# A state-space scan with routed experts on one Trainium2 core: the fifth expert tile one unit later, and x·D by a matmul with a diagonal matrix

## The reference

```python
xn = layernorm(x)
# state-space part, for each batch
x_dbl = xn @ x_proj_w.T                        # 128 + 16 + 16 columns: delta_un, B, C
delta = softplus(delta_un @ dt_proj_w.T + b)   # (512 tokens, 512 channels)
state = exp(delta * A) * state + delta * B * xn    # scan over tokens, 16 states a channel
y     = sum over the 16 states of state * C
s     = y + xn * D_param                       # D_param: one number for each channel
# experts: the 2 of 8 with the largest gate logits, for each token
g     = silu(mean of relu(xn @ expert_w[e] + expert_b[e]) over the two chosen e)
out   = x + s * g
```

## Time and profile before

| | |
|---|---|
| median of 3 runs | 2082.71 us (2080.89 to 2089.23) |
| the profiled execution | 2084.19 us, of which 2082.5 us are the span from first to last instruction |
| mean granted TensorE clock | 0.943 of full |
| busy share of the span | PE 87%, DVE 90%, ACT 73%, POOL 90% |
| batches 1 to 14 | first scan of batch 1 at 190.3 us, of batch 15 at 1946.9 us: 125.5 us each |

### The profile page before, as it was taken

How to read it: one execution, slowest core, us unless ns; L and a number is a source line. 1 busy time by engine, 2 the same in 40 slices (tenths; PEclk the granted TensorE clock), 3 DMA queues, 4 the chain that set the end, 5 groups by cost and what they waited for, 6 DMA issues and landing times.

```text
span 2082.5 us, 30329 instructions
## 1 busy us (share of the span) xinstructions
PE 1812.1 (87%) x8688; PEld 1189.3 (57%) x8688; DVE 1867.7 (90%) x2596; ACT 1517.1 (73%) x3010; POOL 1866.3 (90%) x1004
## 2 busy tenths in 40 slices
PE   4698998989889798998989989798997989889895
PEld 2465655656556465655656556465655656556563
DVE  4777999898999989999898999989989898999997
ACT  4656768687686867768687696867878677686664
POOL 2958999999899999998999999999998999999996
PEclk8798998999999999998999999999999999999997
DMA  8669899898898979889898997979989898998995
GB/s 312 237 200 367 284 312 356 268 383 260 326 331 275 376 243 384 280 298 351 268 377 261 335 342 257 373 246 384 300 283 362 253 364 277 315 347 272 396 308 143
DMA packets 279350, 640.76 MB, mean 308 GB/s; under 512 B 22272, under 2 KB 22784, under 8 KB 268944
## 3 DMA queue, kind: packets, MB, share of 16 engines
q1 hardware_dynamic: 185776, 446.36, 60.9%
q10 hardware_dynamic: 68832, 125.34, 16.2%
q0 software_dynamic: 24576, 67.13, 11.3%
HBM read 516.58 MB, written 122.16 MB: 307 GB/s over the span
## 4 chain that ended last, share of the span: by engine, by line
PE 34%; ACT 18%; DVE 13%; DMA 13%; issue 13%; POOL 6%; SPq 2%; ACTq 1%; DVEq 0%; POOLq 0%
PE z_ps L1214 17%; DMA xn<-in_x 8%; ACT scan_ps L764 5%; DVE scan_ps L1061 5%; PE y_ps L1230 4%; PE proj_ps L1164 4%; POOL dbx L537 3%; DMA bc_rows<-bc_row 3%; DVE p_sb L1071 3%; DVE h_sb L1061 3%; PE y_ps L1247 2%; PE xt_ps L1199 2%; PE proj_ps L1156 1%; ACT xn L623 1%; ACT tok L635 1%
## 5 line engine op out<-in xcount | busy, mean ns | idle before, releaser
L537 POOL TENSOR_TENSOR dbx<-b_sb,u_sb 128x1024 f32<-128x1024 f32 x512 | 1241.9, 2554 | 73.7 <-DVE u_sb L973 37.8
L1214 PE MATMUL z_ps<-w_sb,xsT 128*128 128x512 f32 x1920 | 913.8, 621 | 47.8 <-ACT r_sb L785 25.0
L1061 DVE TENSOR_TENSOR_SCAN scan_ps<-scan_ps,dbx 128x512 f32<-128x512 f32 x704 | 852.9, 1219 | 90.9 <-ACT scan_ps L764 84.8
L764 ACT ACTIVATE scan_ps<-delta,a_sb 128x512 f32<-128x512 f32 x1024 | 699.0, 687 | 213.0 <-DVE p_sb L1071 196.2
L1214 PEld LDWEIGHTS z_ps<-w_sb,xsT 128*128 128x128 f32 x1920 | 363.8, 200 | 432.4 <-issue 423.0
L1230 PE MATMUL y_ps<-ident,p_sb 128*128 128x128 f32 x2816 | 418.3, 283 | 118.6 <-DVE p_sb L1071 118.3
L1230 PEld LDWEIGHTS y_ps<-ident,p_sb 128*128 128x128 f32 x2816 | 336.1, 145 | 244.3 <-DVE p_sb L1071 153.5
L1071 DVE TENSOR_TENSOR p_sb<-scan_ps,c_sb 128x512 f32<-128x512 f32 x704 | 472.0, 671 | 3.0 <-PE y_ps L1230 3.0
L548 POOL TENSOR_TENSOR pp_sb<-h_sb,c_sb 128x1024 f32<-128x1024 f32 (+1 forms) x192 | 411.5, 2143 | 68.2 <-PE y_ps L1247 48.1
L1061 DVE TENSOR_TENSOR_SCAN h_sb<-scan_ps,dbx 128x512 f32<-128x512 f32 x320 | 387.9, 1212 | 64.3 <-ACT scan_ps L764 59.5
L785 ACT ACTIVATE r_sb<-z_ps 128x512 f32<-128x512 f32 x240 | 141.3, 589 | 100.8 <-PE z_ps L1216 95.0
(11 more groups left out here) (134 smaller groups left out, 1437.6 us busy)
## 6 DMA issues: line engine op xcount, KB each, us to landing
w_sb<-in_ew SPq DMA_DIRECT2D x240, 1024.0 KB
b_sb<-bc_rows SPq DMA_DIRECT2D x64, 1024.0 KB, 11.7
ys_rows<-r_sb ACTq DMA_DIRECT2D x240, 256.0 KB
xs<-xs_rows ACTq DMA_DIRECT2D x238, 256.0 KB
c_sb<-bc_rows SPq DMA_DIRECT2D x64, 512.0 KB, 14.1
c_sb<-bc_rows SPq DMA_DIRECT2D x16, 1024.0 KB, 14.9
xo<-in_x SPq DMA_DIRECT2D x64, 256.0 KB, 8.8
out<-acc SPq DMA_DIRECT2D x64, 256.0 KB, 8.8
```

Source lines behind the costliest of these rows:

```text
L537: nc.gpsimd.tensor_tensor(dbx[:, k % DBX_PAIRS], b_sb[:, 2 * m:2 * m + 2, :], u_sb[:, dt % 2, :].unsqueeze(1).to_broadcast([P, 2, T]), ALU ...
L764: nc.scalar.activation(scan_ps[:, bank_of(j), :], delta[:, dt % 2, :], ACT.Exp, scale=a_sb[:, dt, n:n + 1]).then_inc(da_ready, 1)
L1061: nc.vector.tensor_tensor_scan(state, bank, dbx[:, j // 2 % DBX_PAIRS, r % 2, :], 0.0, ALU.mult, ALU.add).then_inc(scanned, 1)
L1214: nc.tensor.matmul(z_ps[:], xsT[:, slot, c, :], w_sb[:, i % WRING, c, :], start=(c == 0), stop=False)
```

## The change

The fifth tile of a batch (number 4, counted from 0) stands at unit 23 in place of 22, in batches 1 to 14. With it its turn goes from unit 18 to 19 on PE, ACT's load of the rows of tile 6 and its `keep_turned` from unit 23 to 24, its relu from 29 to 30. `times_d`, the tile `xD` and the table `XD_AT` are gone. DVE builds four diagonal matrices once at the start, and PE adds x·D by ordinary matmuls of `xT` with these, at the same four places. PE waits there for the copy of x and, in the first batch, for the matrices.

```diff
-XD_AT = {62: 0, 20: 1, 32: 2, 47: 3}
-TILE_AT = {j: i for i, j in enumerate((8, 11, 15, 18, 22, 26, 30, 34, 37, 40, 44, 47, 51, 54, 58))}
+TILE_AT = {j: i for i, j in enumerate((8, 11, 15, 18, 23, 26, 30, 34, 37, 40, 44, 47, 51, 54, 58))}
...
-        xD = sb("xD", [P, T])
+        d_diag = sb("d_diag", [P, DT, P])
...
-            def times_d(b, par, dt):
-                act.wait_ge(proj_used, next_step(b, f"NT{dt}") + 1)
-                act.wait_ge(xd_used, b * DT + dt)
-                nc.scalar.activation(xD[:], xT[:, par, dt, :], ACT.Copy,
-                                     scale=dpar_sb[:, dt:dt + 1]).then_inc(xd_ready, 1)
...
             delta_u(0, 0, 0)
+            for dt in range(DT):
+                nc.vector.tensor_scalar(d_diag[:, dt, :], ident[:], dpar_sb[:, dt:dt + 1], None,
+                                        ALU.mult).then_inc(xd_ready, 1)
...
                 if n == XD_ADD_AT:
-                    pe.wait_ge(xd_ready, k + 1)
+                    pe.wait_ge(proj_used, next_step(b, f"NT{dt}") + 1)
+                    if is_first(b):
+                        pe.wait_ge(xd_ready, DT)
                     for tt in range(TT):
-                        last = nc.tensor.matmul(y[:, tt, :], xD[:, tt * P:(tt + 1) * P], ident[:],
-                                                start=False, stop=False, is_transpose=True,
-                                                skip_group_check=True)
+                        last = nc.tensor.matmul(y[:, tt, :], xT[:, par, dt, tt * P:(tt + 1) * P], d_diag[:, dt, :],
+                                                start=False, stop=False, skip_group_check=True)
                     last.then_inc(xd_used, 1)
```

More of the change, by code:

```diff
@@ L691, in copy_t @@
                     act.wait_ge(u_ready, from_start((b - 1) * DT))
-                    act.wait_ge(xd_ready, from_start((b - 1) * DT))
+                    act.wait_ge(xd_used, from_start((b - 1) * DT))
                 nc.scalar.activation(xT[:, par, dt, :], proj_ps[:], ACT.Copy).then_inc(proj_used, 1)
@@ L838, in _ @@
             keep_delta(0, 0)
-            times_d(0, 0, 0)
             act.wait_ge(a_ready, 1)
@@ L895, in batch @@
                         keep_delta(b, int(name[1]))
[L896 to L899, removed]
                     if j - EVAC_LAG in tiles:
@@ L1217, in tile, with add_y @@
                                  start=False, stop=True).then_inc(z_done, 1)
-            def add_y(b, j):
+            def add_y(b, par, j):
                 dt, n = j // N, j % N
@@ L1286, in batch @@
                     if on_dve(j):
-                        add_y(b, j)
+                        add_y(b, par, j)
                     if j % QUAD == 2:
```

## The result

The changed kernel takes **2106.36 us** (median of 4 runs, 2097.66 to 2112.99) beside 2082.27 us of the kernel before (4 runs of the same session, 2080.89 to 2089.23): ratio 1.0099, 95% interval 1.0073 to 1.0126. By the medians it is 24 us slower, by the interval 15 to 26, where 47 were forecast. The profiled execution is 2104.11 us (span 2102.4), 20 us above that of before.

The account below looks back on a forecast made before the run. PE was taken as the bound from NT1 to unit 38. Tile 31, unit 49 9, unit 33 6 and edges 1 sum to 47 us on 2084.2, so 2131; predicted 2130 us, 2.3% slower, 8 in 10 within 2094 to 2150.

Parts of the forecast that it names:

- Part 1, the tile: Units 20 to 38: the turn of tile 4 behind tile 3 makes PE 2.2 us late a batch, +31 us.
- The rival in which PE's lateness sinks before unit 38: Units 29 to 38 absorb PE's lateness; only 21 us remain, 2104 us; chance 0.14.
- The group of x·D: Eight matmul records for four transposes on PE, at four places: 0.65 us more each, between 0.44 and 0.97.
- unit 33: The longer x·D group delays the turn of tile 9 and ACT's load: 0.4 us a batch, +6 us.
- unit 17: The longer x·D group lies in PE's 1.20 us idle before NT1: nothing, 0.2 us at the most.
- Unit 49: The longer x·D group delays ACT's relu and the scan of unit 57: 0.65 us in 14 batches, +9 us.
- a rival in which the change adds a loss: PE's clock falls around tile 4, between units 20 and 28: 25 us on top, 2155 us; chance 0.08.
- The edges: Batches 0 and 15: the x·D groups at units 33 and 49 cost up to 0.65 us each, +1 us.
- DVE's four scalings: Done once where DVE waits for the first batch's routing counts: nothing, 3 us at the most.

Follow-up runs that it names:

- e15: Kernel before with the tile at unit 23, x·D as before, plus 12 transposes of zeros on PE ahead of NK: 2101.74 us.
- e11: Kernel before plus 12 transposes of zeros on PE ahead of NK in batches 1 to 14: 2067.85 us.
- e3: Changed kernel with the turn of tile 4 back at unit 18, ahead of tile 3: 2093.54 us.
- e4: Kernel before with the turns of tiles 5 and 6 each done twice in batches 1 to 14: 2098.42 us.
- e9: Changed kernel with ACT's load of tile 6's rows and the copy behind it at unit 25 for 24: 2099.42 us.
- e1: Kernel before with only the tile moved to unit 23, x·D as before: 2103.28 us.
- e6: Changed kernel run again unchanged, for a second trace: 2100.60 us (1 run).
- e14: Changed kernel plus 12 transposes of zeros on PE ahead of NK: 2103.51 us.
- e16: Kernel before with only x·D on PE, the tile at unit 22, plus 12 transposes of zeros ahead of NK: 2072.65 us.
- e2: Changed kernel with the tile at unit 22 again, so only x·D on PE is new: 2096.05 us.
- e5: Kernel before with one extra, unused DVE reduction of 0.671 us at unit 62 of 14 batches: 2087.83 us.
- e13: Kernel before run again unchanged, for a second trace: 2094.79 us (1 run).
- e12: Kernel before with ACT's copy of NT0 at unit 21 for 22, plus 12 transposes of zeros ahead of NK: 2054.52 us.
- e10: Changed kernel with ACT's copy of NT0 at unit 21 for 22: 2108.75 us.

## Why the prediction was half right

**Part 1, the tile: right.** Scan 24 idles 2.93 us (3.1 forecast), scan 28 doesn't wait, the turn of tile 4 holds the load on ACT (868.28, where the forecast moved by the start of NT1 has 868.33), NT3 starts behind an idle 0.72 (0.9), PE is 2.14 us late at the turn of tile 8 (2.2), scan 38 waits 2.63 (2.8). 14 × 2.2 = 31 us were forecast, 14 × 2.19 are in the table, and e15 - e11 is 33.9. e3 and e4 show that PE's unbroken run is what carries it, e9 that half of it comes by way of the blocked load. The rival in which PE's lateness sinks before unit 38 falls with every batch of the five traces that have the tile at 23 and its turn behind tile 3 (after, e1, e6, e14, e15: 38.9 us or more from scan 20 to scan 38), though its time, 2104, was nearest to the result: a right time for a wrong reason.

**The group of x·D: the low end of its range.** 0.65 us was taken, between 0.44 and 0.97. Two neighbouring starts give it, batch 6 after:

```profile
897.47 1.06 PE L1231 MATMUL y_ps<-d_diag,xT 128*128 128x128 f32 x8
```

The next instruction starts at 898.36, 0.89 behind it, where the four transposes took 0.44: 0.45 more, 0.11 a record. At unit 33 it cost 0.30 to 0.38 us a batch (0.4 forecast), at unit 17 nothing, as long as the copy of NT0 stands at 22.

**Unit 49: the step that failed.** The +9 us stood on "another unbroken run of PE, at whose end ACT's relu waits 0.48 us at 925.17". That row is from batch 6, a low batch. With full clock the scan of unit 57 waits for next to nothing, and units 41 to 57 take 28.1 us with either x·D: the term is 0. In low batches it is 0.6 us (29.2 against 29.8), nearly what was forecast. One batch was read as all 14. With unit 33's 6 us, x·D was forecast at 15 us, and e16 - e11 is 4.8.

**The clock: the term that was missing.** Rows 10 showed 1.2 GHz behind NK, and it was used only for a rival in which the change adds a loss. It was not asked in how many batches it falls (8 of 14), what that costs (1.1 us up to unit 57 and 0.7 more in the next batch), or whether it would stay so. The changed kernel has it in 1 and 0 batches, e1 in 2, against 7 to 12 in the five traces with tile and copy at 22 (before, e2, e4, e5, e13) and 9 in e3. Seven low batches fewer, at 1.8 us, are 13 us, near what filling showed (12.3). The 19 us of the first table are nearly all clock: in the trace of the kernel before, units 0 to 6 take 10.94 us behind a low batch and 9.57 behind another, so there a low batch costs 2.5 us, and seven of them 17. The change's own lateness, which shortens the wait for x, gave back little: behind batches that are not low these units take 9.57 us before and 9.42 after, 2 us in 14 batches. So the distance from 47 to 24 is 12 us of clock and 11 us at equal clock (47 - 35.7), of which unit 49 is 9.

**The edges** were put at 1 us, and the traces can't tell. In e14 to e16 batch 0 is 5 to 6 us longer than in e11, but so it is in e12 (145.0 us), which has neither half of the change, and batch 1 of e11 is 5 to 8 us longer than theirs, in its units 0 to 6 (19.6 us), where ACT waits 10.6 us for x. Executions differ there by more than the edits do. DVE's four scalings were nothing, as forecast: the first scan comes at 45.9 us, before at 45.8.

**A term of single executions: the start.** The first scan comes at 45.8 to 46.8 us in nine of the 18 traces and at 51.1 to 52.1 in the other nine; the kernel before is in both groups (45.8, and 51.2 in e13). PE's pace tells them apart. The last eight records of the first projections, in the kernel before and then in e2:

```profile
30.34 1.41 PE L1164 MATMUL proj_ps<-xwg_sb,xT 128*128 128x168 f32 x8
...
32.99 2.61 PE L1156 MATMUL proj_ps<-xwg_sb,xT 128*128 128x168 f32 x8
```

They take 1.41 us in all nine early traces and 2.6 in all nine late ones. The records of the granted clock begin at 27 to 28 us in the early traces and only behind the first scan in the late ones, so that the slow half of the start is read from these durations. 5 us are worth as much as three low batches, and profiled executions are to be compared with that in mind.

**Left open.** Why the clock falls behind the same 1.8 us of idle in one batch and not in the next, and why less often with the tile at 23, no run settles: e9 and e10, also with the tile at 23, have 5 and 6. Nor is it settled why PE is slow at the start in some executions, or why ACT waits 8 to 11 us for x in batch 1 of some (e1, e4, e6, e11). The unfilled changed kernel's runs spread over 15 us, and two traces with 1 and 0 low batches do not explain that. That a low batch's 0.7 us in the next one runs through a later load of x was only argued.

## What to carry to other kernels

Before a stall of one iteration goes into a sum, look for the same place in other iterations: if the granted clock or the stall differs between them, there are two kernels to predict, and the change may also move the share of each. Where a stall is removed ahead of an engine's unbroken run, the gain is paid back at the end of the run; move the start of the run instead (13 us in 14 batches at equal clock, e12 against e11). And a DMA issue that waits in an engine's program blocks this engine's arithmetic as any instruction does: when a producer moves behind a long instruction, move what waits for it too.

## What the runs showed of the hardware

An idle of 1.8 us on PE was enough for the granted clock to fall from 2.4 to 1.2 GHz behind it, but not each time: 8 of 14 batches in one execution of the kernel before, 12 of 14 in another. With the idle cut to 0.51 us by 12 transposes of zeros it fell there in none of 70 batches (e11, e12, e14 to e16), and the spread of the changed kernel's runs went from 15 us to 3. The Trainium skill (TensorE: Matmul & The Clock Gate, Part 4: PE-mode transpose) says that the full clock doesn't engage for transposes, which don't count as PE being busy in the same way. By that rule these should have changed nothing, and the 15 us of e11 speak against it. The same page (Part 1: The HAM clock gate) says of the slow matmuls at the start of a kernel that their number differs between runs. The 1.41 and the 2.6 us at the start agree, and the 8 and the 12 low batches show the same of a place in the middle.

An ordinary float32 matmul of 128 columns is two records and 0.22 us from start to start, a transpose of the same shape one record and 0.11 us, so x·D by a diagonal matrix costs PE twice what adding a finished product costs.
